# An expert-stage kernel whose first two units take their rows from three of four batches

## What is computed

```python
h = _layernorm(x, axis=-1) * (1 + cb) + sb
logits = x_flat @ w_router.T
probs = jax.nn.softmax(logits, axis=-1)
top_idx = jnp.argmax(probs, axis=-1)
h = jnp.einsum('nd,ehd->enh', x_flat, w_fc)
a = jnp.square(jnp.where(h >= 0, h, 0.5 * h))
expert_out = jnp.einsum('enh,edh->end', a, w_proj)
out = jnp.einsum('end,en->nd', expert_out, mask * top_weight[None, :])
x = x + gb * out
```

## Time and profile before

| what | value |
|---|---|
| median of 3 runs | 567.5 us (566.24 to 568.49) |
| the profiled execution, its own time | 567.73 us |
| its span | 566.0 us |
| granted clock of TensorE, mean | 0.962 |
| TensorE busy | 513.0 us, 91% |
| VectorE busy | 346.0 us, 61% |
| ScalarE busy | 264.4 us, 47% |
| GpSimd busy | 145.2 us, 26% |
| mean DMA rate | 78 GB/s |

### The profile page before, as it was taken

The page is one execution under the profiler, slowest core; times in us unless marked ns, Lnnn a source line. Parts: engine busy times, 40 slices in busy tenths (PEclk is TensorE's granted clock), DMA queues, the critical chain, the costliest instruction groups (busy, mean ns, idle before and its releaser), DMA issues.

```text
span 566.0 us, 7661 instructions
## 1 busy us (share of the span) xinstructions
PE 513.0 (91%) x2280; PEld 391.0 (69%) x2280; DVE 346.0 (61%) x724; ACT 264.4 (47%) x524; POOL 145.2 (26%) x161
## 2 busy tenths in 40 slices
PE   7899899997438999999999999999999999999960
PEld 1454355635227788888888889888888888988850
DVE  4588999897768665545454446444554535546780
ACT  2664386846577653443353344344245334432310
POOL 1000013221204330050033033025005203634883
PEclk9899999997868999999999999999999999999995
DMA  8920342220503001222022003002202200143995
GB/s 298 426 96 5 144 150 75 76 76 1 149 1 77 3 2 58 96 75 75 2 76 76 1 13 138 2 1 75 77 1 75 76 1 1 61 111 100 154 122 73
DMA packets 15009, 44.19 MB, mean 78 GB/s; under 512 B 5017, under 2 KB 5017, under 8 KB 11625
## 3 DMA queue, kind: packets, MB, share of 16 engines
q1 hardware_dynamic: 10600, 34.71, 17.5%
q0 software_dynamic: 4352, 8.69, 8.6%
HBM read 34.94 MB, written 8.71 MB: 77 GB/s over the span
## 4 chain that ended last, share of the span: by engine, by line
PE 73%; DVE 13%; ACT 6%; issue 3%; DMA 1%; POOL 1%; ACTq 1%; DVEq 0%; SPq 0%; POOLq 0%
PE bank L1060 33%; PE bank L1034 32%; DVE xc L1166 3%; ACT XSfull L682 2%; PE bank L925 2%; PE bank L884 1%; PE bank L898 1%; PE bank L929 1%; DMA x_in<-x 1%; DVE st L1148 1%; DVE res L1204 1%; POOL out L551 1%; ACT XSfull L686 1%; PE bank L908 1%; PE bank L877 1%
## 5 line engine op out<-in xcount | busy, mean ns | idle before, releaser
L505 POOL TENSOR_TENSOR Wlo<-raw,Whi x56 | 70.6, 1290 | 239.7 <-ACT Whi L807 239.7
L1034 PE MATMUL bank<-XShi,Whi 128*128 x320 | 115.1, 360 | 9.7 <-ACT XShi L783 9.7
L1469 DVE TENSOR_TENSOR acc<-acc,bank 128x512 f32<-128x512 f32 x119 | 81.1, 687 | 62.6 <-PE bank L1060 62.6
L1034 PE MATMUL bank<-XSlo,Whi 128*128 x320 | 115.0, 359 | 0.0
L1034 PE MATMUL bank<-XShi,Wlo 128*128 x320 | 115.0, 359 | 0.0
L1453 DVE TENSOR_TENSOR twice_h<-twice_h,bank 128x512 f32<-128x512 f32 (+2 forms) x80 | 48.3, 607 | 100.5 <-ACT twice_h L792 100.5
L1060 PE MATMUL bank<-Whi,ahi 128*128 128x512 f32 x272 | 106.1, 390 | 2.3 <-DVE alo L1459 2.3
L1060 PE MATMUL bank<-Wlo,ahi 128*128 128x512 f32 x272 | 106.1, 390 | 0.0
L1060 PE MATMUL bank<-Whi,alo 128*128 128x512 f32 x272 | 106.0, 390 | 0.0
L801 ACT ACTIVATE ahi<-twice_h 128x512 fp32r<-128x512 f32 (+2 forms) x80 | 45.4, 568 | 122.5 <-PE bank L1060 122.5
L792 ACT ACTIVATE twice_h<-bank 128x512 f32<-128x512 f32 (+2 forms) x80 | 42.4, 530 | 90.2 <-PE bank L1034 80.8
(11 more groups left out here) (169 smaller groups left out, 539.8 us busy)
## 6 DMA issues: line engine op xcount, KB each, us to landing
raw<-wffn SPq DMA_DIRECT2D x16, 1024.0 KB, 5.2
wm<-wmod SPq DMA_DIRECT2D x6, 1024.0 KB, 13.1
out<-res SPq DMA_DIRECT2D x4, 1024.0 KB, 4.5
x_in<-x SPq DMA_DIRECT2D x3, 1024.0 KB, 12.9
ga_bc<-ga_rows SPq DMA_DIRECT2D x4, 256.0 KB, 3.7
x<-x SPq DMA_DIRECT2D x1, 1024.0 KB, 5.1
bc<-router_rows_scaled SPq DMA_DIRECT2D x4, 256.0 KB, 3.5
wx_sb<-wx SPq DMA_DIRECT2D x1, 514.0 KB, 8.7
```

What stands on the lines that cost most here:

```text
L505: pool.tensor_tensor(Wlo[:, hb % 2, c, :], raw[:, c, :], Whi[:, hb % 2, c, :].bitcast(F32), ALU.subtract).then_inc(s_wlo, 1)
L1034: mm = pe.matmul(hP[(par + u) % 2][m][:, c0:c1], W[wp][:, par, 2 * e + k // 2, o:o + P], XS[xp][:, k, bass.ds(start_row[u] + c0, c1 - c0)] ...
L1469: dve.tensor_tensor(acc[:, n, :], acc[:, n, :], yP[s][:, :], ALU.add).then_inc(s_yu, 1)
```

## The change

**Assignment in two steps.** `assign_first` runs on VectorE after the sort of batch 2 and gives units 0 and 1: one from the front if expert 0 has by then rows enough for it (`least` against the running count), else from the back. `assign_rest` gives the other three after the sort of batch 3.

**Units 0 and 1 first.** `XShi` and `XSlo` of unit 0 are made before batch 3 is placed, and `fc` of unit 0 runs before its blocks are turned, `fc` of unit 1 behind them. ScalarE places blocks 0 and 1 of batch 3 between the Relu and the squares of unit 0, and blocks 2 and 3 behind the squares; VectorE places in the same halves. `proj` of unit 0 waits for all of batch 3, whose blocks now use the four banks that `proj` writes. The third unit's rows are split one job later than before.

**Around it.** Blocks 0 and 1 of batch 2 are turned after three of batch 3's four outputs, blocks 2 and 3 behind the fourth, ahead of `prefix(3)`. `guess2(3)` moves from behind the third placement of batch 2 to behind the second. The first four `Wlo` move on VectorE from ahead of batch 3's residuals to behind its margins; the other four go to GpSimd. The last `top_weight`, and with it the last scatters, move behind the placement of batch 3. `perm` moves in memory, and the margin products of batch 3 write their unused product elsewhere.

```diff
-        place_bank = [(pT[0], pT[1], pT[0], pT[1])] * (NB - 1) + [(pT[0], pT[1], pC, pD)]
+        place_bank = [(pT[0], pT[1], pT[0], pT[1])] * (NB - 1) + [(pD, pX, pO[0], pO[1])]
...
+                if b == NB - 1:
+                    pool.wait_ge(s_wlo, CH // 2)
+                    for c in range(CH // 2, CH):
+                        low(0, c)
...
-            place(2, (0, 1, 2))
+            place(2, (0, 1))
             guess2(3)
-            place(2, (3,))
-            normalize2(3)
-            margin_exp(3)
-            act.wait_ge(s_x2, TJ * NB)
-            split_first(range(4, 6))
-            place(NB - 1)
-            act.wait_ge(s_e0, KT * NBLK)
-            act.wait_ge(s_e1, TJ * (NB - 1))
-            act.wait_ge(s_e1d, KT * TJ)
-            act.wait_ge(s_unit, 2)
+            place(2, (2, 3))
...
+            act.wait_ge(s_early, 2)
+            act.wait_ge(s_e0, KT * TJ * (NB - 1))
+            act.wait_ge(s_e1, TJ * (NB - 1))
+            act.wait_ge(s_y, TJ * NB)
+            high_rows(0)
+            normalize2(3)
+            margin_exp(3)
+            high_rows(1)
+            act.wait_ge(s_x2, TJ * NB)
+            split_first(range(4, CH))
...
-                for n in between:
-                    high_rows(n)
+                for what, n in between:
+                    what(*n)
...
-            high_rows(0)
-            high_rows(1)
-            split_first(range(6, CH))
             for u in range(NU):
-                job(0, 0, u, (u + 2,) if u + 2 < NU else ())
+                if u == 0:
+                    job(0, 0, 0, ((place, (NB - 1, (0, 1))),))
+                    place(NB - 1, (2, 3))
+                    act.wait_ge(s_e0, KT * NBLK)
+                    act.wait_ge(s_e1d, KT * TJ)
+                    act.wait_ge(s_unit, 2)
+                else:
+                    job(0, 0, u, ((high_rows, (u + 1,)),) if u + 1 < NU else ())
...
-                if b < NB - 1 or j < 2:
+                if b < NB - 1:
                     wait(pe, s_e0, KT * (n - 1))
+                else:
+                    pe.wait_ge(s_rk, NB)
+                    pe.wait_ge(s_x2, TJ * NB)
...
                 for j in ORDER[:3]:
                     state_output(b, j)
+                if not nxt:
+                    permuted_block(b - 1, 0)
+                    permuted_block(b - 1, 1)
                 if b > 0:
                     skip_product(b, 0)
                 state_output(b, 0)
+                if not nxt:
+                    permuted_block(b - 1, 2)
+                    permuted_block(b - 1, 3)
...
-                else:
+                elif nxt:
                     permuted_block(b - 1, 0)
                     permuted_block(b - 1, 1)
...
+                if b > 0 and nxt:
+                    permuted_block(b - 1, 2)
+                    permuted_block(b - 1, 3)
...
-                if b > 0:
-                    permuted_block(b - 1, 2)
-                    permuted_block(b - 1, 3)
...
-            for j in range(TJ):
-                permuted_block(NB - 1, j)
...
+            start_row, pick = [], []
+            def load_unit(u):
+                start_row.append(pe.value_load(startI[0:1, u:u + 1], min_val=0, max_val=ROWS - P * UNITS[u]))
+                pick.append(pe.value_load(pickI[0:1, u:u + 1], min_val=0, max_val=2))
...
+            pe.wait_ge(s_early, 2)
+            load_unit(0)
+            load_unit(1)
+            fc_weights_ready(0)
+            pe.wait_ge(s_e0, KT * TJ * (NB - 1))
+            fc(0, 0, 0, landing=True)
+            for j in range(TJ):
+                permuted_block(NB - 1, j)
+            pe.wait_ge(s_x2, TJ * NB)
+            pe.wait_ge(s_xhi, KT * 2)
+            pe.wait_ge(s_xlo, KT * 2)
+            fc(0, 0, 1)
+            proj_weights_ready(0)
+            pe.wait_ge(s_e0, KT * NBLK)
+            pe.wait_ge(s_e1d, KT * TJ)
+            proj(0, 0, 0)
             pe.wait_ge(s_unit, 2)
-            start_row = [pe.value_load(startI[0:1, u:u + 1], min_val=0, max_val=ROWS - P * UNITS[u]) for u in range(NU)]
-            pick = [pe.value_load(pickI[0:1, u:u + 1], min_val=0, max_val=2) for u in range(NU + 1)]
-            fc_weights_ready(0)
-            for u in range(NU):
...
+            for u in range(2, NU):
+                load_unit(u)
+            pick.append(pe.value_load(pickI[0:1, NU:NU + 1], min_val=0, max_val=2))
+            for u in range(2, NU):
+                pe.wait_ge(s_xhi, KT * (u + 1))
+                pe.wait_ge(s_xlo, KT * (u + 1))
+                fc(0, 0, u)
+                proj(0, 0, u - 1)
...
-            def assign_units():
-                dve.wait_ge(s_vec, 3 * NU)
+            def assign_first():
+                dve.wait_ge(s_vec, 3 * NU + 5)
+                own.link(dve.tensor_scalar(front[:, 0:2], least[:, :], run[:, 0:1], None, ALU.is_ge))
+                dve.tensor_scalar(pickI[:, 0:2], front[:, 0:2], -2.0, 2.0, ALU.mult, ALU.add).then_inc(s_early, 1)
+                start_rows(0, 2, s_early)
...
+            def start_rows(u, n, ready):
+                own.mark(dve.tensor_tensor(startf[:, u:n], front[:, u:n], reach[:, u:n], ALU.mult))
+                own.link(dve.tensor_tensor(taken[:, u:n], front[:, u:n], width[:, u:n], ALU.mult))
+                own.link(dve.tensor_tensor_scan(ends[:, u:n], ones[:, u:n], taken[:, u:n], ends[:, u - 1:u] if u else 0.0,
+                                                ALU.mult, ALU.add))
+                own.link(dve.tensor_tensor(startf[:, u:n], ends[:, u:n], startf[:, u:n], ALU.subtract))
+                own.link(dve.scalar_tensor_tensor(startf[:, u:n], startf[:, u:n], float(P), behind[:, u:n], ALU.mult, ALU.add))
+                dve.tensor_copy(startI[:, u:n], startf[:, u:n]).then_inc(ready, 1)
...
+            def assign_rest():
...
+                own.link(dve.tensor_reduce(total[:, 0:1], begun[:, :], mybir.AxisListType.X, ALU.add))
+                own.link(dve.tensor_tensor(rest[:, 0:1], total[:, 0:1], ends[:, 1:2], ALU.subtract))
+                own.link(dve.tensor_scalar(level[:, :], level[:, :], rest[:, 0:1], None, ALU.is_le))
+                own.link(dve.tensor_tensor(over[:, :], level[:, 1:2], level[:, 2:3], ALU.subtract))
+                own.link(dve.tensor_tensor(front[:, 2:3], level[:, 0:1], over[:, :], ALU.subtract))
+                own.link(dve.scalar_tensor_tensor(rest[:, 0:1], front[:, 2:3], -4.0, rest[:, 0:1], ALU.mult, ALU.add))
...
+                dve.tensor_scalar(pickI[:, 2:NU + 1], front[:, 2:NU + 1], -2.0, 2.0, ALU.mult, ALU.add).then_inc(s_unit, 1)
+                start_rows(2, NU, s_unit)
...
+                    if b == NB - 1:
+                        assign_first()
...
-                else:
-                    lows(range(4))
...
+            lows(range(4))
+            ranks(NB - 1)
+            permutations(NB - 1)
             low_rows(0)
+            assign_rest()
             low_rows(1)
-            lows(range(4, CH))
+            dve.wait_ge(s_e1, TJ * (NB - 1))
             for u in range(NU):
                 twice(0, 0, u)
-                if u + 2 < NU:
-                    low_rows(u + 2)
+                if u == 0:
+                    place_from_back(0)
+                    place_from_back(1)
+                elif u + 1 < NU:
+                    low_rows(u + 1)
                 if u > 0:
                     accumulate("first", 0, u - 1)
                 low(0, u)
+                if u == 0:
+                    place_from_back(2)
+                    place_from_back(3)
+                    dve.tensor_scalar(gapI[:, :], tokF[:, 0:1], n0f[:, 0:1], None, ALU.add).then_inc(s_n0, 1)
+                    top_weight(NB - 1)
```

57 lines of the change are left out of this document (18 added, 39 removed).

## The result

The changed kernel takes **558.42 us** (median of 4 runs, 557.73 to 559.35), the kernel before beside it 567.09 (566.24 to 568.49): ratio 0.9842, 95% interval 0.9821 to 0.9864. That is 8.7 us less. Forecast were 4.5 less (563.2), with a range down to 560.6: the direction is right, the size is off by nearly half, and the range is missed. Two more comparisons of the same kernel gave 0.9835 (0.9815 to 0.9854) and 0.9836 (0.9817 to 0.9854), that is 9.3 us less, so about 9 us it is. The profiled execution took 557.73, with a span of 555.9.

What follows compares the result with a forecast made beforehand. TensorE was taken as the bound from the first second-layer product on, with two chains racing to its start. The sum -6.65 + 2.16 = -4.5 us gave 563.2 us, own range 562.0 to 564.7, overall 560.6 to 567.0.

Steps and rivals of the forecast that it cites:

- Step 1: Start of batch 3's sort: earlier batch 2 blocks and guess end the margins at 153.6, not 155.57, 1.95 us earlier.
- Step 2: From the margins to the first expert product: Wlo, ranks, permutations, then XSlo; TensorE starts at 158.95, before at 171.25.
- Step 3: First unit and batch 3's placement: placement is the later chain, first second-layer product at 178.3, not 184.95, giving 6.65 us.
- Step 5: GpSimd's Wlo beside VectorE's XSlo of unit 1: memory contention taken as 0, given about 2 us of VectorE slack.
- the other end, +1.2: Upper bound for GpSimd and VectorE taking turns at memory: 3.9 us less slack of 2 and 0.7, +1.2 us.
- Step 4: TensorE's clock: a 4.2 us hole before the first second-layer unit starts that unit at 1.2 GHz, +2.16 us.
- +2.16: First second-layer unit's cost at the fallen clock: 7.60 us instead of 5.44.
- what else moves has room: Moved work off the chain around the seam: fits without cost, with XSlo of unit 1 done by 166.1, wanted at 168.65.
- first rival: Gap before the first second-layer unit: clock holds, so the full 6.65 us is gained, 561.1 us; chance 0.20.
- the sort did start earlier: Rival for batch 3's sort: it does not start earlier, margins stay at 155.57, chain 1.95 later, 565.2 us; chance 0.10.
- the seam did not run at half clock throughout: Rival for TensorE's seam: clock stays at half throughout, +2.5 us, 570.2 us, slower; chance 0.08.
- third rival: Seam: both engines collide and the clock returns late, one or two of +1.2, +1.4, +1.4, around 565.8 us; chance 0.17.

Runs made afterwards that it cites:

- e2_order_back: Changed kernel with `mod_rows(5)` put back ahead of blocks 2 and 3 of batch 1: 562.03 us, ratio 0.9896 to the kernel before.
- e9_sort_late: Changed kernel with batch 2's blocks 0 and 1 turned behind the fourth output again and the guess after three placements: 559.75 us, ratio 0.9867.
- e8_sort_alone: Kernel before plus the `mod_rows(5)` swap, batch 2's early blocks and the guess after two placements, without early units: 561.51 us, ratio 0.9902.
- e3_gpsimd_later: Changed kernel with GpSimd's four Wlo subtractions held until unit 1's XSlo are written: 558.10 us, ratio 0.9837 to the kernel before.
- e4_registers_early: Changed kernel with TensorE's seven register loads ahead of its wait for the placement: 557.50 us, ratio 0.9828 to the kernel before.
- e7_all_filled: Changed kernel with GpSimd's Wlo later, register loads early, and unread products filling TensorE's gaps before the first unit and first second-layer products: 555.75 us, ratio 0.9797.
- e5_before_filled: Kernel before with four unread products in TensorE's 4.2 us gap ahead of the skip products: 565.26 us, ratio 0.9958.
- a0_after_again: Changed kernel unaltered, measured again beside the kernel before: 558.08 us, ratio 0.9835.
- a1_after_third: Changed kernel unaltered, measured a third time beside the kernel before: 558.25 us, ratio 0.9836.

## Why the prediction missed the size

**Step 1 failed, and twice.** It priced two moves in the loop of the batches (the blocks 0 and 1 of batch 2, the guess) and put a third at nothing without a reason, or even a mention: the swap of `mod_rows(5)` with the blocks 2 and 3 of batch 1. Priced from the trace of before, it would have read: 3.60 us of TensorE go behind blocks that ScalarE had waited 8.02 us for, so ScalarE is earlier by up to 3.6, the margins of batch 2 too, and the gap of 4.2 us that the earlier trace rows name as the cause of the half clock closes. Measured at m(3): 3.1 and 2.9 us; at the end 5.0 in the profile, 4.9 (3.7 to 6.0) by the runs. Second, the 1.95 us that it did price hold only without the swap. In e2_order_back the margins' last step starts at 153.41 where 153.6 was forecast as the end, and m(3) is 2.5 earlier than before, 0.5 better than priced (the moved Wlo has a part in this that no run separates); with the swap, the same moves are worth 0.6 (e9_sort_late) or nothing (e8_sort_alone).

**The priced parts came out near their sum in the profile, by offsetting errors.** e2_order_back is the kernel that the prediction in fact described. It was forecast at 4.5 us under before; its profile is 4.3 under (457.1 against 461.4), its runs 5.9 (4.9 to 6.9). This profile's m(1) is 0.5 us later than that of before, so the forecast's times are best compared as distances from m(1), forecast ones from 104.57. Its chain, which lists of each step only the part that it passes through (the last line is cut at the end of the view):

```profile
163.31 1.31 DVE startf L1337
164.64 0.33 DVE startI L1338
...
169.73 0.68 DVE XSlo L1486
...
179.18 5.73 PE bank L1086 x24
184.91 1.15 issue
186.06 4.14 PE bank L1060 x17
```

- *Step 2* holds: first product at 158.71, forecast 158.95. From m(1) that is 53.65 against 54.38, 0.7 better, and 0.5 of it is step 1's.
- *Step 3* is 1.1 short: from the first product to the first second-layer product it has 19.35 us (158.95 to 178.3), and 20.47 were taken (158.71 to 179.18). The second unit was to end at 174.1, and ended near 178: its XSlo took 4.63 us and were done 4.3 us later than the 166.1 in "what else moves has room". That sentence was wrong.
- *Step 5* was mis-sized. It charged 0 by a slack of 2 us on VectorE. It counted on big operations alone; beside GpSimd's Wlo two steps on 128x3 elements took 1.30 and 1.22 us here, and three took 1.18 to 1.23 in the changed kernel. The slack was used up, and the other end, +1.2, is what e3_gpsimd_later measures (1.1 to 1.25). By the rule of the Trainium skill, SBUF — State Buffer, section Who interferes with whom, the sum would have been the one with +1.2: e3_gpsimd_later agrees.
- *Step 4* had the mechanism right and the place wrong. The late second unit shrank the forecast gap from 4.2 to 1.05 us, and the +2.16 wasn't paid there. The clock fell one unit earlier instead, in the second unit, behind a wait of 3.12 us for its rows (granted clock 1.00 in the wait, 0.70 from 170.79 to 174.0): this unit took 7.34 us, against 5.73 with the clock up (e4_registers_early), and that stood beside the placement, which was the later chain. Where the gap stays long, 4.09 us in e3_gpsimd_later, the clock falls in it, and that costs 2.7. The prediction named this link under its first rival (if VectorE takes turns, the gap shrinks) and still gave it 0.20.
- *Missing altogether*: seven register loads of TensorE, which were hidden in the hole before the first expert product and now stand between the first second-layer unit and the third unit: 1.03 us in the changed kernel, 1.15 here. The diff shows the move. From the first second-layer product to the third unit it took 6.88 us, 1.3 more than the 5.58 of before.
- *Behind the seam* another 0.7 us were lost (from the third unit on 376.1 us, before 375.5), which no step had.

-0.7 + 1.1 - 2.16 + 1.3 + 0.7 = +0.2: errors that cancel, which is luck. Step 3's picture, the placement as what the first second-layer product waits for, is right in every profile with the early units but e7_all_filled, whose unread products end just as late.

The rivals: the sort did start earlier; the seam did not run at half clock throughout; the clock held in the first second-layer unit in one of three profiles of the changed kernel, and fell in the other two. Not every wait was followed by a fall: behind 1.13 us (the kernel after) and 2.40 us (e4_registers_early) the unit ran at full clock throughout. Of the third rival the collision came, with its 1.2 us, but the time stayed far below its 565.8.

**What stays open.** Why the clock falls behind the same waits at 164.8 in one run of the changed kernel and at 173.9 in the next is not settled. The difference between the profile (4.3) and the runs (5.9) of e2_order_back wasn't taken apart, so how near the priced parts came to 4.5 stays open by 1.6 us. The moves of `perm` and of the last `top_weight` were never run by themselves. That e7_all_filled gave nothing more on the median may be that early stretch rather than the seam; one profile can't tell.

## What to carry to other kernels

Price every line of the diff, above all a change in the order of calls that looks like a by-product: put each moved operation beside who waits for it in the trace before. Where two gains act on the same wait, work out the second with the first in place. And where an engine's gap costs the clock, making one feeder faster can lengthen the gap and give the gain back: fill the gap, or shift both.

## What the runs showed of the hardware

- Unread products in a gap pay: 3.6 us of them gave 2.4 us (e5_before_filled), since TensorE's clock stayed at its 2.4 GHz level for 6.8 us (1.00) in which it had been at 1.2 GHz (0.50 in the earlier trace rows).
- VectorE steps on 128x3 elements took 1.18 to 1.30 us beside GpSimd's subtractions of 128x512, and 0.16 to 0.17 without them: seven times as long, and about the length of one GpSimd subtraction (1.26 in the earlier trace rows). Even the conversion with a single input was hit. In e2_order_back the step at 163.11 still took 0.16 us, and the two behind GpSimd's start at 163.29 took 1.30 and 1.22.
- The other way is seen, though no run tests it. Beside VectorE's Wlo a small GpSimd step took 1.82 us in the kernel after, where it had taken 0.34 with no Wlo beside it in the kernel before (the last line):

```profile
147.60 0.64 POOL L499 TENSOR_TENSOR pos<-m,back 128x4 f32<-128x4 f32 x1 [5.11 <-DVE m L1290]
148.22 1.82 POOL L500 TENSOR_SCALAR cand<-m,pback,tokF 128x4 f32<-128x4 f32 x1
```

```profile
155.77 0.34 POOL L493 TENSOR_SCALAR cand<-m,pback,tokF 128x4 f32<-128x4 f32 x1
```

- Seven register loads on TensorE's queue leave a hole of 1.03 to 1.15 us behind a unit that ran at full clock throughout (5.73 to 5.75 us), and none to speak of behind one that took 7.3 us or more (a0_after_again, a1_after_third, e9_sort_late, e3_gpsimd_later). Unit and hole together are 6.8 to 6.9 us, which is an estimate of how long the loads take beside the products.
